# A vision layer on one core: the last image's expert weights fetched in pairs, in steps 5 to 12 of the last phase

## The reference, cut to what matters

```python
# 1. token mixing, per image
h = prelu(((d_gamma * (q @ k.T)) @ v) @ Wo + bo)
# 2. a state scan with 16 states for each of 128 channels, over the 1024 tokens
x_conv = silu((h @ W_in_main) @ W_conv + b_conv);  B, C = split(x_conv @ W_bc + b_bc)
dt = softplus(x_conv @ W_dt + b_dt)
state_t = exp(dt_t * A) * state_(t-1) + (dt_t * x_conv_t) * B_t
y_t = sum over the 16 states of state_t * C_t
h = layernorm(h + (y * silu(gate)) @ W_out + b_out)
# 3. two expert layers: every group of 64 tokens has one expert of 16, chosen by route_id
f = relu(h @ Wi.T + bi)
for l in range(2):
    f = relu(shared_l(f) + (f @ Wr[l, expert_of_group].T + br[l, expert_of_group]) + f)
out = layernorm(h + f @ Wo.T + bo)
```

## Time and profile before

| | |
|---|---|
| median of 3 runs | 335.23 us (334.68 to 344.01) |
| the profiled execution | 334.67 us |
| its span (first to last instruction) | 332.9 us |
| PE busy | 274.3 us (82% of the span) |
| DVE busy | 264.8 us (80%) |
| POOL busy | 256.7 us (77%) |
| ACT busy | 191.6 us (58%) |
| DMA queue q1 (SP's) | 84.42 MB, 76.5% of the 16 engines' span |
| `late` copies, gam<-expert_w | 16 of 128 KB, median 5.2 us from issue to landing |

### The profile page before, as it was taken

How to read it: one execution, slowest core, us unless ns; L and a number is a source line. 1 busy time by engine, 2 the same in 40 slices (tenths; PEclk the granted TensorE clock), 3 DMA queues, 4 the chain that set the end, 5 groups by cost and what they waited for, 6 DMA issues and landing times. The chain is left out here.

```text
span 332.9 us, 4726 instructions
## 1 busy us (share of the span) xinstructions
PE 274.3 (82%) x1454; PEld 156.9 (47%) x1454; DVE 264.8 (80%) x289; ACT 191.6 (58%) x300; POOL 256.7 (77%) x134
## 2 busy tenths in 40 slices
PE   7899918875778589999889789997695787997996
PEld 4423402333435244346564243464564656765674
DVE  3465687998768898998798989998898887999711
ACT  2103931326895433478967354689738686888253
POOL 0009037999999998998999989999998689999500
PEclk9999976999798879999999899999969799999999
DMA  7980297587779999767699997676999999998301
GB/s 234 410 318 0 50 335 293 185 261 248 254 269 265 316 295 398 257 239 278 209 318 289 321 345 269 232 248 228 312 275 318 344 275 342 324 340 297 97 0 32
DMA packets 46889, 85.88 MB, mean 258 GB/s; under 512 B 7697, under 2 KB 24593, under 8 KB 46609
## 3 DMA queue, kind: packets, MB, share of 16 engines
q1 hardware_dynamic: 46464, 84.42, 76.5%
q10 hardware_dynamic: 400, 1.17, 1.3%
HBM read 75.62 MB, written 1.57 MB: 232 GB/s over the span
## 5 line engine op out<-in xcount | busy, mean ns | idle before, releaser
L1254 POOL TENSOR_TENSOR hc<-h,c_row 128x1024 f32<-128x1024 f32 (+1 forms) x79 | 154.4, 1963 | 16.9 <-DVE h L1383 13.8
L1243 POOL TENSOR_TENSOR ub<-u,b_row 128x1024 f32<-128x1024 f32 (+1 forms) x47 | 95.6, 2034 | 15.7 <-DMA b_row<-bc_dram 14.9
L951 ACT ACTIVATE decay<-delta,neg_a 128x512 f32<-128x512 f32 (+1 forms) x62 | 49.9, 815 | 65.4 <-DVE h L1383 65.2
L684 PEld LDWEIGHTS acc_y<-pack,hc 128*128 128x128 f32 x512 | 61.3, 149 | 47.9 <-issue 27.5
L684 PE MATMUL acc_y<-pack,hc 128*128 128x128 f32 x512 | 75.7, 289 | 9.9 <-POOL hc L1254 6.2
L1383 DVE TENSOR_TENSOR_SCAN h<-decay,ub 128x512 f32<-128x512 f32 (+1 forms) x40 | 64.9, 1621 | 15.4 <-POOL ub L1243 10.7
L626 PE MATMUL work<-q,kT 64*128 64x512 f32 x112 | 34.9, 702 | 17.8 <-DVE mixed L1409 13.5
L1409 DVE TENSOR_TENSOR mixed<-gam,work 128x512 f32<-128x512 f32 x56 | 35.6, 676 | 7.3 <-PE work L626 6.6
L978 ACT ACTIVATE decay<-u 128x512 f32<-128x512 f32 (+1 forms) x44 | 27.8, 639 | 20.7 <-DVE h L1383 20.4
L637 PE MATMUL acc_r<-mixed,v_sb 128*64 128x512 f32 x128 | 37.0, 658 | 1.1 <-DVE mixed L1409 1.0
L1383 DVE TENSOR_TENSOR_SCAN h<-decay_own,decay 128x512 f32<-128x512 f32 (+1 forms) x24 | 35.7, 1487 | 1.2
(11 more groups left out here) (226 smaller groups left out, 353.4 us busy)
## 6 DMA issues: line engine op xcount, KB each, us to landing
b_row<-bc_dram SPq DMA_DIRECT2D x64, 512.0 KB, 5.3
c_row<-bc_dram SPq DMA_DIRECT2D x64, 512.0 KB, 5.4
group_w<-expert_w SPq DMA_DIRECT2D x48, 128.0 KB, 4.7
gam<-gammaT SPq DMA_DIRECT2D x8, 512.0 KB, 10.4
expert_w<-routed_w SPq DMA_DIRECT2D x1, 2048.0 KB, 18.4
gam<-expert_w SPq DMA_DIRECT2D x16, 128.0 KB, 5.2
x_in<-xT SPq DMA_DIRECT2D x4, 256.0 KB, 9.2
pack<-packed ACTq DMA_DIRECT2D x1, 788.0 KB, 7.4
```

What stands on the lines that cost most here:

```text
L684: mm = nc.tensor.matmul(acc_y[:, to:to + P], hc[:, at:at + P], ident, start=(job.state == 0 and c % 4 == 0), stop=(job.state == STATES - 1 ...
L951: op = nc.scalar.activation(target, delta[:, job.image % 2, columns], ACT.Exp, scale=neg_a[:, job.state:job.state + 1])
L1243: nc.gpsimd.tensor_tensor(ub[:, ring(made, job.halves)], u[:, job.image % 2, tokens(q)], b_row[:, ring(job.at, job.halves)], ALU.mult).the ...
L1254: nc.gpsimd.tensor_tensor(hc[:, here], h[:, here], c_row[:, here], ALU.mult).then_inc(hc_ready, job.halves)
```

## The change

The 16 look-ups and copies of the last image's expert weights are issued in other steps. Before, step n of phase 3 has the copy of group n, for n = 0 to 15. Now steps 0 to 4 and 13 to 15 have none, and steps 5 to 12 have two each: groups 2n - 10 and 2n - 9. Groups 0 to 7 are therefore copied in steps 5 to 8 and groups 8 to 15 in steps 9 to 12. What is copied, where to, its size and its semaphores stay as they are.

```diff
-                    if p == ALONE:
-                        look_up_group(p, n)
-                        load_late_group(n)
+                    if p == ALONE and 5 <= n < 13:
+                        for g in (2 * n - 10, 2 * n - 9):
+                            look_up_group(p, g)
+                            load_late_group(g)
```

## The result

| | before | after |
|---|---|---|
| median | 334.89 us (6 runs) | 336.42 us (6 runs, 335.88 to 341.85) |
| the profiled execution | 334.67 us | 336.20 us |
| its span | 332.9 us | 334.4 us |

The ratio is 1.0049, with an interval of 1.0033 to 1.0065: slower by 1.6 us (1.1 to 2.2). The forecast was 336.0. All ratios in this document leave out executions in which the core was disturbed, while the medians include them.

The account below looks back on a forecast made before the run. DMA engines bound the start of phase 3, POOL the rest. Waits of +2.46 us less 1.54 won gave +0.9 at 6.0 us landing, +1.3 at the 6.2 taken: 334.67 + 1.3 = 336.0 us; range 333.0 to 338.7.

Parts of the forecast that it names:

- the relief: Copies gone from steps 0 to 4: POOL's gaps of 0.96 and 0.58 us in phase 3 vanish, -1.54 us.
- the waits: POOL waiting for late B rows from step 11 on, +2.46 us in sum at a landing time of 6.0 us.
- What it adds: A second look-up and copy ahead of the B rows of steps 9 to 15, 1.30 us of SP's time each.
- T: Time from a B row's issue to its landing in phase 3: 6.0 us at first, 6.2 us taken.
- The walk: Step-by-step timing of B rows 11 to 15: POOL waits 1.86, 0.08, 0.07, 0.36 and 0.1 us.
- What the change takes away: Copies of steps 0 to 4: B rows issued some 1.4 us earlier, two POOL gaps gone, -1.54 us.
- What it moves elsewhere: Copies of steps 13 to 15 go to steps 10 to 12 and earlier; counted as nothing.
- Only the relief shows: Rival: the 1.54 us are won and the second copies cost nothing, 333.1 us; chance 0.25.
- Nothing shows: Rival: early gaps come from `bc_dram` read latency and B rows have more room, 334.7 us; chance 0.13.
- Delay that feeds on itself: Rival: pairs fill the DMA engines in steps 9 to 15, landing time 9.0 us, 341.6 us; chance 0.04.

Follow-up runs that it names:

- The relief alone: Kernel before with no copy in steps 0 to 4, one each in steps 5 to 12, the rest behind the last B row: 1.0033, repeated 1.0001.

## Why the prediction was right

**The outcome.** 336.0 us were forecast and 336.42 measured; +1.3 us, and +1.6 by the ratio. The mechanism forecast, B rows issued late by SP's time and landing after POOL wants them, is the one that the runs show. Two terms inside the sum were off, the relief and the waits, and cancelled in part; that the number came out so near is in part luck. In the two traces, from the `ub` behind the first gaps to the end, the change costs 2.8 us, and the spans differ by only 1.5 because that execution came to this `ub` 1.3 us sooner. A second measurement had 2.3 to 5.6 us.

**"What it adds", SP's time.** Right. The second look-up and copy took 1.31 us (1.94 - 0.63), against 1.30 forecast. The distance from C row to B row was 3.28 us and not 3.10: the C row's own issue now takes 0.5 us in place of 0.36, and the look-up behind it starts later. SP's step came to 3.9 us against 3.77. That SP's time ahead of the B row costs by itself is shown by the kernels with the time and no more bytes (1.0082, and 1.0156 with twice the time), by the same time elsewhere (0.9986) and, on the chip of the first, by the bytes without the time (1.0010). That it isn't all, the kernel with small copies shows: with T at 4.5 us its trace has 0.94 us of late gaps.

**The walk.** At step 11, 1.86 us were forecast; the trace has 1.12 us ahead of this `ub` and 0.74 just before, ahead of an `hc`, 1.86 together. That this is the same number to the digit is luck. The second half of it I had not seen: I walked B rows only, while the C row is late as well, since SP issues it behind the B row. Behind that the forecast was small waits of 0.08, 0.07, 0.36 and 0.1 us; the trace has 0.42, 0.22, none and 1.32; the second large one came at step 15 and not at step 14. The sum forecast was 2.46 us, that of the trace 3.82 (second trace 2.46). The size of single gaps varies by more than I can forecast.

**T, the landing time.** I took 6.2 us, expecting it to rise with the DMA share. The share did fall ahead of 276 us, to 1.00, and rise in the last stretch, to 1.01, but the median stayed at 6.0 us. The bytes do count: T is 4.5 us with small copies, and three rows took 7.2 to 7.6 us where SP's pace did not hold the rows back. That SP issues too slowly in the kernel after for a queue to build up is how I read it; it fits the 4.6 us of the kernel with twice the SP time, but no run tests it alone.

**"What the change takes away", 1.54 us.** This is the term that failed. I read two gaps of one trace as a fixed sum that the copies cause. Without a copy the B row follows its C row after 0.66 us (266.86 to 267.52) in place of 1.80, so it is issued 1.1 us earlier and not 1.4; that is still more than either gap. The relief alone gave ratios of 1.0033 and 1.0001, whose intervals exclude 1.5 us, and no copies at all 0.9997, at most 1.2 us. The second trace of the relief alone has 1.16 us of the same gaps, with B rows at 8.1 us and no copy near. So the relief is between nothing and 1.1 us, and with the 1.6 us of the ratio the pairs cost between 1.6 and 2.7 us in the first measurement, where my sum had 2.8 (1.3 + 1.54).

**"What it moves elsewhere."** Nothing, as forecast: from POOL's last `hc` to the end of the span are 20.0 us (314.36 to 334.4), against 20.1 before.

**The rivals.** *Only the relief shows* gives the time that the skill's rule gives. The Trainium skill, "DMA: Bandwidth & Descriptors", section "Issuing engines are not separate DMA queues", calls the time to initiate a transfer usually small beside the transfer. Beside the 5.2 us in which a copy landed before, the 1.3 us are small, as the page has it; beside the 0.41 us of the engines' time (an estimate) they are not. What decided is what stood behind them: ahead of a row on which POOL waits, 1.2 us of look-ups a step cost 0.8% with no byte more to move. *Nothing shows* had the better ground for the relief, since such gaps came without any copy near, and the wrong one for the pairs. *Delay that feeds on itself* did not occur: T stayed at 6.0 us with the pairs, and with twice the SP time and no pairs it fell to 4.6.

## What to carry to other kernels

Transfers issued by one engine are a serial program. Before a cheap transfer is put into it, ask which issue stands behind it, how much room that one has from landing to use, and whether the engine waits anywhere else in the step: the same look-ups cost 0.8% ahead of the B row and, on another chip, nothing measurable behind it. A ring of three steps looks like much room, but its refill waits for the consumer's progress, and 0.1 to 0.8 us were left here. And a gap of half a microsecond in one trace is not yet a gain to be had: leave the suspected work out altogether and time that first. And two traces are compared from a mark ahead of the change's reach: here that mark moved by up to 3.8 us between executions, more than the effect sought.

## What the runs showed of the hardware that I had not expected

The same 512 KB rows landed after 4.0 to 9.0 us, by the traffic around them: 4.5 us in the median with small copies, 6.0 with full ones, 8.1 in a stretch at a DMA share of 1.03 that had no copies but two stores. SP's issue of a C row took 0.36 us where it had waited for POOL and 0.46 to 0.54 where it followed a B row's issue directly; single B rows took up to 1.4 us to issue. The change cost 0.5% in one set of runs and 1.2% in another, with intervals that don't overlap.
